# Who sends the row of score maxima in the causal attention layers: ScalarE instead of SyncE

## The reference

```python
# block 0: causal attention with ALiBi
scores = einsum('bhtd,bhsd->bhts', q, k) / sqrt(D) + slopes * pos
attn = softmax(where(causal, scores, -inf)); y = einsum('bhts,bhsd->bhtd', attn, v)
x = x + (y.reshape(b, t, c) @ w_proj + b_proj)
# block 0: 4 experts, each an attention over the tokens routed to it (top 2), per batch
att = softmax(where(validg, q @ k.T * 0.5, -1e9)); out[order] += wg * ((att @ v) @ wo[e] + bo[e])
# block 1: causal attention with rotary positions
x = x + attention(rope(q), rope(k), v) @ Wo.T
# block 1: a shared expert and 64 small experts, top 8 per token
```

## Time and profile before

| what | value |
|---|---|
| three runs | 4254.94, 4249.04, 4247.9 us, median 4249.04 us |
| profiled execution | 4240.4 us |
| span of its trace | 4238.6 us |
| PE busy | 3488.5 us (82%) |
| DVE busy | 2386.4 us (56%) |
| ACT busy | 2099.9 us (50%) |
| POOL busy | 886.0 us (21%) |
| TensorE clock, mean granted | 0.91 |

### The profile page before, as it was taken

The page is one execution under the profiler, slowest core; times in us unless marked ns, Lnnn a source line. Parts: engine busy times, 40 slices in busy tenths (PEclk is TensorE's granted clock), DMA queues, the critical chain, the costliest instruction groups (busy, mean ns, idle before and its releaser), DMA issues.

```text
span 4238.6 us, 57105 instructions
## 1 busy us (share of the span) xinstructions
PE 3488.5 (82%) x21603; PEld 1679.5 (40%) x21604; DVE 2386.4 (56%) x3494; ACT 2099.9 (50%) x4557; POOL 886.0 (21%) x686
## 2 busy tenths in 40 slices
PE   4899999758898989898898877663498888889895
PEld 2445445323323333333333333332244434435574
DVE  3565656637474747474564544322567797785523
ACT  1566666436565656565565544331165545453221
POOL 1223422320101010101011011112333232110374
PEclk8999999979999999999999999776699989899897
DMA  4644445331313130303213143233343232203488
GB/s 126 190 144 136 134 124 174 96 104 33 82 27 83 27 86 24 90 21 85 65 45 79 29 108 99 70 90 101 104 115 109 74 100 78 66 23 121 117 201 224
DMA packets 332971, 403.27 MB, mean 95 GB/s; under 512 B 43994, under 2 KB 301386, under 8 KB 325773
## 3 DMA queue, kind: packets, MB, share of 16 engines
q1 hardware_dynamic: 280606, 344.53, 28.9%
q0 software_dynamic: 18432, 35.67, 3.6%
q10 hardware_dynamic: 33664, 19.53, 2.0%
HBM read 233.12 MB, written 156.96 MB: 92 GB/s over the span
## 4 chain that ended last, share of the span: by engine, by line
PE 57%; DVE 19%; DMA 6%; issue 6%; ACT 4%; POOL 3%; ACTq 2%; SPq 2%; PEldq 0%; POOLq 0%; PEld 0%; DVEq 0%; another core or an unknown queue 0%
PE PSUM L773 14%; DVE M L1002 11%; PE PSUM L733 11%; PE PSUM L751 10%; PE PSUM L678 6%; PE PSUM L795 3%; PE PSUM L714 2%; PE PSUM L592 2%; ACTq L555 2%; DVE best L1348 2%; DVE XR L1351 2%; DMA qk_d<-PH 1%; ACT P L943 1%; PE PSUM L781 1%; POOL xg_d L1392 1%
## 5 line engine op out<-in xcount | busy, mean ns | idle before, releaser
L1002 DVE TENSOR_REDUCE M<-PSUM 128x1 f32<-128x896 f32 (+7 forms) x1704 | 1704.0, 1032 | 1103.5 <-PE PSUM L733 669.5
L943 ACT ACTIVATE P<-PSUM 128x512 f32<-128x512 f32 (+2 forms) x3520 | 1580.7, 503 | 841.8 <-PE PSUM L751 510.9
L751 PE MATMUL PSUM<-QS,KS 101*128 101x512 bf16 (+2 forms) x3520 | 1080.8, 345 | 101.9 <-ACT P L943 57.3
L733 PE MATMUL PSUM<-KS,QS 99*128 99x512 bf16 (+3 forms) x3600 | 943.7, 345 | 255.1 <-issue 100.6
L773 PE MATMUL PSUM<-P,VA 128*17 128x384 f32 (+3 forms) x7040 | 788.3, 524 | 6.6 <-ACT P L943 6.6
L751 PEld LDWEIGHTS PSUM<-QS,KS 101*128 101x128 bf16 x3520 | 332.2, 99 | 845.3 <-ACT P L943 452.4
L644 POOL TENSOR_TENSOR QF<-QF,PH 128x1024 f32<-128x1024 f32 (+4 forms) x98 | 157.5, 1607 | 2040.2 <-ACT PH L898 2001.0
L733 PEld LDWEIGHTS PSUM<-KS,QS 99*128 99x128 bf16 x3600 | 319.1, 100 | 667.2 <-DVE M L1002 284.0
L678 PE MATMUL PSUM<-XT,W 128*128 128x512 f32 (+2 forms) x672 | 305.0, 582 | 8.5 <-DMA bq<-in_L_ffn_bk 4.3
L773 PEld LDWEIGHTS PSUM<-P,VA 128*17 128x17 f32 x7040 | 137.1, 97 | 248.7 <-issue 207.2
L736 PE MATMUL PSUM<-identb,maskB 128*128 128x128 bf16 x1024 | 217.8, 227 | 0.0
(11 more groups left out here) (199 smaller groups left out, 3070.2 us busy)
## 6 DMA issues: line engine op xcount, KB each, us to landing
qk_d<-PH SPq DMA_DIRECT2D x120, 256.0 KB
xg_d<-GX SPq DMA_DIRECT2D x19, 1152.0 KB, 11.5
yg_d<-GX SPq DMA_DIRECT2D x17, 1152.0 KB, 9.1
XF<-xg_d SPq DMA_DIRECT2D x18, 1024.0 KB, 7.7
VA<-n_L_ffn_expert_gate_up_w SPq DMA_DIRECT2D x64, 256.0 KB, 3.5
QS<-qk_d SPq DMA_DIRECT2D x36, 384.0 KB, 6.2
KS<-qk_d SPq DMA_DIRECT2D x36, 384.0 KB, 5.6
qk_d<-PH SPq DMA_DIRECT2D x48, 224.0 KB
```

What stands on the lines that cost most here:

```text
L733: mm = e.matmul(slot_heads(s, hb)[:, x, a:b], QS[0:KA, g, h + x, 128 * qt:128 * qt + 128], KS[0:KA, g, h + x, a:b], start=True, stop=not d ...
L751: mm = e.matmul(s[:, 0:q1 - q0], KS[0:KB, g, j, 128 * kt:128 * kt + 128], QS[0:KB, g, j, q0:q1], start=True, stop=not diag, skip_group_che ...
L943: e.activation(P[:, m % NP, 0:q1 - q0], s[:, 0:q1 - q0], ACT.Exp, scale=ly.scale).then_inc(S["act_p"], 1)
L1002: e.tensor_reduce(m[:, qt, h:h + hb], v[:, :, 0:kn], AX.X, ALU.max).then_inc(S["dve_a"], 1)
```

## The change

In the causal layers `mr` moves from SP's list to ACT's, directly behind the copy `mt` that fills `MR`. Its two DMAs go through ACT's DMA queue, as in the units. ACT must wait for its own copy to be complete (`act_a`) before it issues them. The wait for the second pass of the batch before (`pe_s`) is written for ACT too. SP's branch is removed.

```diff
@@ attention_act @@
-                elif kind == "mr" and moe:
+                elif kind == "mr":
                     g = task[2]
                     w.wait_ge("act_a", "mt", i, g)
-                    if O.ahead(i):
+                    if not moe:
+                        w.wait_ge("pe_s", "s2", i - 1, g, O.layer.nch - 1, O.layer.nt - 1, 3)
+                    elif O.ahead(i):
                         w.wait_ge("pe_s", "s2", i - 1, g, O.layer.nch - 1, O.layer.nt - 1, 3)
                     row_of_maxima(e, ly, g)
@@ attention_sp @@
-                elif kind == "mr" and not moe:
-                    g = task[2]
-                    w.wait_ge("pe_s", "s2", i - 1, g, ly.nch - 1, ly.nt - 1, 3)
-                    w.wait_ge("act_a", "mt", i, g)
-                    row_of_maxima(e, ly, g)
```

## The result

The changed kernel takes 4297.33 us (median, 4290.14 to 4309.3); the kernel before, on the same chip, 4248.47. The ratio is 1.0122, with a 95% interval of 1.0093 to 1.015. That is 49 us slower, where I had forecast 7 and a range up to 4268. The profiled execution took 4290.14 us, span 4288.3.

A forecast was written before the change was run, and what follows sets the result against it. PE's program order was taken as the path. ACT's issues +25.7, waiting places -5.05, clock -5.1, first group -6.0 and end of `l0` -2.5 gave +7.05 us; +7 on 4249.04 made 4256 us, range 4240 to 4268.

The forecast's parts named there:

- the change part by part: The forecast's list of effects in `l0` and `l1`, beginning with SP's release and summing to +7.05 us.
- worth nothing by itself: SP loses 66 issues, about 41 us, and its waits for ACT; off the path in general, so no gain.
- I take about 0.1, as ACT's queue holds nothing else there: Remaining landing wait at each of four `l0` groups where PE waited: possible 0 to 0.65 us, taken as about 0.1.
- the five rivals: Five competing totals for the whole kernel: 4256 (chance 0.42), 4259 (0.12), 4268 (0.10), 4269 (0.12), 4239 us (0.24).
- Rival 2: The row of maxima's landing does not get quicker on ACT's queue: 4259 us; chance 0.12.
- ACT's cost: In `l0` and `l1`, ACT's issues delay its next exponential and PE, mostly 1.1 us per place; 25.7 us over 27 places.
- The four waiting places: Four `l0` groups where PE waits for the row: 9.9 us saved against 4.4 and 0.45 paid, net -5.05 us.
- the recovered clock: With shorter waits in `l0` the clock no longer falls behind late rows: -5.1 us, bounds 0 and 7.4.
- The first group: In `l0`'s first group ACT issues the row 4.85 us earlier than SP did; taken as -6.0 us.
- the bound between 4.85 and 6.6: Possible gain in `l0`'s first group: 4.85 us from earlier issue, up to 6.6 with a quicker landing.
- The end of `l0`: Residual load and POOL's bias addition come earlier, so the output store does too: -2.5 us, bounds -4 and 0.
- The sum: All terms over the kernel: 25.7 - 5.05 - 5.1 - 6.0 - 2.5 = +7.05 us, giving 4256 us.

The follow-up runs named there:

- run 4: Changed kernel, ACT sends the row of maxima, but SP waits at its old place until the row has landed; ratio 1.0041, 4267.81 us.
- run 5: Kernel before, SP still sends the row; in the causal layers ACT also issues an equal pair to an unread DRAM tensor; ratio 1.0034, 4305.99 us.
- run 8: Changed kernel, but in the causal layers ACT sends only the first of two rows and SP the second at its old place; ratio 1.0018.
- run 6: Kernel before, but in `l1` SP's store of Q's parts and next `QS` load stand just ahead of the row in each batch's first group; ratio 1.0011.
- run 7: Kernel before, but in `l0` each batch's third-group `KS` load and the first unit's mask stand just behind the row; ratio 0.9987.
- run 11: The same kernel as run 7, measured once more against the kernel before; ratio 0.9994.

## Why the prediction was wrong

**The failed step** is the first of "the change part by part": SP's release is "worth nothing by itself". I priced what SP no longer does, and not what it now does sooner. SP's stop at `mr` had kept its stores, loads and zeroings behind the row of maxima. Freed, it sends them as soon as their own waits end, and in `l1` a load then starts 1.2 to 2.1 us ahead of the copy's end in four groups, and a store and the residual load 4.7 to 6.9 ahead in a fifth. In `l0` the fifth and the fourteenth group (landings of 6.5 and 6.7 us, 3.1 before; 4.7 and 5.6 us longer) pay most: in the fifth a load of `KS`, the residual load and a zeroing start 2.8 to 1.0 us ahead of the copy's end, in the fourteenth the zeroings of `ye_d`. The loss by this is 15.8 us in `l1` and 10.5 in `l0`, run 4 against after. The same error stands once more in "I take about 0.1, as ACT's queue holds nothing else there": I looked at the queue and not at the transfers in flight, and PE still waits 1.14 us in the ninth group and 2.65 in the thirteenth. None of the five rivals had a landing that gets *later*. Rival 2 is the nearest, but it left the landing where it was.

**ACT's cost, right.** Exponential 1.30 behind the copy, normal group +1.09, `l1` +13.9 in run 4 against 13. Runs 5 and 8 show that the price of a normal group goes with the issue time. That the sum for `l1` came out so near is in part luck: two groups cost far more than forecast (below) and others less.

**The four waiting places and the recovered clock, too hopeful by a third.** The four are the seventh, ninth, thirteenth and sixteenth group, where PE waited 0.3, 2.9, 3.2 and 3.5 us. In run 4 the seventh is 0.8 us longer, the others 1.7, 2.8 and 3.3 shorter: net -7.0, clock included, against -5.05 and -5.1. In the changed kernel it is +0.7, -1.4, +0.6 and -3.2: net -3.3. The clock term did show in the stretches of the ninth and the sixteenth group, at 1.00 now (0.96 and 0.93 in the earlier trace rows), but the fifth, which was at 1.00, is at 0.96. Single groups vary by up to 2.2 us between executions of the same code, so these sizes are rough.

**The first group, too hopeful.** 3.6 us instead of 6.0; the bound between 4.85 and 6.6 had not allowed for a landing of 5.9 with the zeroing and the store in flight.

**The end of `l0`, right**: -2.3 against -2.5.

**The sum.** With run 4 in place of the change, 1.0041 (17 us, 10 to 25 by its interval) stands against the 7 forecast: nearer, but still more than I had. The profile of before was also a favourable one: 4240.4, where the kernel before had a median of 4245.91 and reached down to 4232.26 and up to 4263.71 over the runs on the first chip (one of 25 took 8513.19 and is left out of the ratios); 9 us of this lie between the seventeenth and eighteenth copy.

**The Trainium skill** (DMA: Bandwidth & Descriptors, "Issuing engines are not separate DMA queues") has DMAs of several issuers run on the same DMA engines and interleave. The trace agrees, and more strongly than I had used it: with a load from SP's queue in flight the row lands after 7 us instead of 2.5. The same page ("Queues, rings and completion order") has each DMA engine take turns between queues by packets, from which I had read some shelter for a small transfer on a queue of its own. No shelter shows: at equal lead of the load the row lands at 4.8 us from ACT's queue and at 4.4 to 5.1 from SP's.

**Left open.** Why a load whose lead is a microsecond shorter delays the row by 2.5 us more was seen, not taken apart. The lead alone does not decide it: in the third group of `l1` a load 1.7 us ahead gave 4.0 us, less than 2.1 ahead in the first. In the first, fifth and ninth group gathers of POOL, the last of them issued 2.2 to 2.3 us ahead of the copy's end, are in flight besides, in the third none; before, with the same gathers and no load, the row landed at 2.64. Two groups of `l1` with a granted clock under 0.9 (from the seventh and the eleventh copy) lost 2.4 to 2.8 us each in after and in run 4, against next to nothing in the forecast; DVE is busy in 53 of 65.5 us there, so PE is not the only path. The sum for `l1` came out right because others cost less.

## What to carry to other kernels

A queue that waits is also a gate: before a wait is taken off an engine, list what stands behind it, and ask what these transfers will be in flight with. A small transfer on which the critical engine waits should go out ahead of the large ones (here 0.76 us and more ahead was in time, together with them or behind them was not), from whichever engine is idle. And an engine that feeds the critical one without pause should issue no DMAs: here each issue was paid nearly in full, and where the issues went the granted clock rose as well. Here moving them off it in the units gave 2.1%, by the change's own mechanism read backwards.

## What the runs showed of the hardware

The issue of a DMA cost ACT more for one target than for the other: 0.30 us each from `MR` to DRAM (run 5), 0.6 from `MR` to `QS` (after), for the same 8 KB.

On the second and third chip every kernel stands still in `l0` while POOL issues its sixteen scattering DMAs: in run 6 the groups that end with the ninth, thirteenth and seventeenth copy are 18.9, 19.9 and 12.3 us longer than before on the first chip, where POOL issues the same sixteen without such a pause. At the seventeenth copy that leaves 40.9 us, most of the 48 by which the chips differ. From the timeline of run 6:

```profile
420.85 0.69 DVE L1004 TENSOR_REDUCE M<-PSUM 128x4 f32<-128x512 f32 x1 [14.58 <-issue]
...
421.60 0.50 PE L735 MATMUL PSUM<-KS,QS 99*128 99x384 bf16 x1 [8.73 <-DVE M L1004]
...
430.01 1.57 ACT L945 ACTIVATE P<-PSUM 128x512 f32<-128x512 f32 x3 [13.07 <-remote]
```

DVE is idle 14.58 us without a releaser that the trace shows, then ACT 13.07. The cause stays open. In the ninth and thirteenth group it also took away the late landings that runs 7 and 11 were to remove, so that a difference measured on one chip need not hold on another.
